# One gathered tile in twenty-four is built by ScalarE from columns of the node table, in both layers of a graph network

## The reference

```python
# layer 0, then x = layernorm(x + y)
m = relu(concat([x[dst], x[src], edge_attr, u[batch[dst]]]) @ W1.T + b1)
y = relu(concat([x, segment_sum(m, dst), u[batch]]) @ W2.T + b2)
# layer 1, then x = layernorm(x + y)
h = relu(concat([x[src], x[dst], edge_attr]) @ msg_w1 + msg_b1)
a = segment_mean(h @ msg_w2 + msg_b2, dst)
y = relu(concat([x, a]) @ upd_w1 + upd_b1) @ upd_w2 + upd_b2
```

## Time and profile before

| | us |
|---|---|
| median of 3 runs (lowest, highest) | 3929.26 (3928.97, 3930.61) |
| span of the profiled execution | 3929.8 |

### The profile page before, as it was taken

How to read it: one execution, slowest core, us unless ns; L and a number is a source line. 1 busy time by engine, 2 the same in 40 slices (tenths; PEclk the granted TensorE clock), 3 DMA queues, 4 the chain that set the end, 5 groups by cost and what they waited for, 6 DMA issues and landing times.

```text
span 3929.8 us, 45222 instructions
## 1 busy us (share of the span) xinstructions
PE 3229.0 (82%) x16881; PEld 2975.7 (76%) x16881; DVE 1583.8 (40%) x3640; ACT 590.4 (15%) x1017; POOL 2960.2 (75%) x3156
## 2 busy tenths in 40 slices
PE   6988888888788888888878888878888888888887
PEld 6877777777777777777778777777777777777776
DVE  6533334343444444444543333333433333333333
ACT  1211111111111111111111111111111111111111
POOL 7777777777777777777777777777777777777776
PEclk7755555565655556665665555555555555555556
DMA  7644444444444444445454444444444444444443
GB/s 261 200 138 134 135 136 143 132 133 139 148 139 149 149 149 147 147 147 154 131 158 135 133 131 124 135 139 136 139 136 141 139 142 137 140 135 141 142 142 100
DMA packets 257760, 563.18 MB, mean 143 GB/s; under 512 B 131254, under 2 KB 151713, under 8 KB 232572
## 3 DMA queue, kind: packets, MB, share of 16 engines
q1 hardware_dynamic: 132824, 332.20, 25.4%
q0 software_dynamic: 100032, 205.00, 19.8%
q10 hardware_dynamic: 24676, 23.01, 1.7%
HBM read 537.29 MB, written 22.66 MB: 142 GB/s over the span
## 4 chain that ended last, share of the span: by engine, by line
POOL 70%; issue 23%; DMA 4%; DVE 2%; PE 2%; ACT 0%; SPq 0%; POOLq 0%; DVEq 0%
POOL Qr L319 70%; DMA Qr<-tabQ,srcE 3%; DVE BIG L1405 1%; PE bank L1137 0%; DMA srcE<-in_srcL 0%; DVE BIG L1302 0%; PE bank L1119 0%; PE bank L1092 0%; DVE BIG L1392 0%; DMA tabQ<-BIG 0%; DVE BIG L1400 0%; PE bank L1051 0%; PE bank L1045 0%; DVE AC L609 0%; POOL Qr L325 0%
## 5 line engine op out<-in xcount | busy, mean ns | idle before, releaser
L319 POOL DMA_INDIRECT Qr<-tabQ,srcE x3094 | 2925.3, 945 | 942.9 <-issue 933.2
L1137 PE MATMUL bank<-BIG 128*128 128x42 f32 x6252 | 1379.0, 396 | 143.6 <-ACT BIG L1287 141.1
L1119 PE MATMUL bank<-wall,BIG 128*128 128x128 f32 x6252 | 1473.0, 410 | 19.1 <-DMA BIG<-tabP 19.1
L1137 PEld LDWEIGHTS bank<-BIG 128*128 128x128 f32 x6252 | 1307.5, 308 | 207.6 <-ACT BIG L1287 201.5
L1302 DVE TENSOR_TENSOR BIG<-bank,BIG 126x512 bf16<-126x512 f32 x782 | 539.3, 690 | 2264.7 <-DMA Qr<-tabQ,srcE 2254.8
L1119 PEld LDWEIGHTS bank<-wall,BIG 128*128 128x128 f32 x6252 | 1311.5, 309 | 23.8 <-issue 23.8
L1287 ACT ACTIVATE BIG<-BIG 128x512 f32<-128x512 f32 (+1 forms) x782 | 492.1, 629 | 3229.1 <-DVE BIG L1405 3220.4
L1124 PE MATMUL bank<-BIG 126*128 126x128 bf16 x3126 | 490.2, 295 | 506.5 <-DVE BIG L1302 396.7
L1124 PEld LDWEIGHTS bank<-BIG 126*128 126x128 bf16 x3126 | 342.0, 135 | 639.0 <-DVE BIG L1302 455.9
L1405 DVE TENSOR_TENSOR BIG<-bank,Qr 128x512 f32<-128x512 f32 (+1 forms) x782 | 532.7, 681 | 41.2 <-PE bank L1124 25.3
L1392 DVE TENSOR_TENSOR BIG<-bank,relE 128x168 f32<-128x168 f32 x782 | 252.6, 323 | 3.5 <-DMA Qr<-tabQ,srcE 3.5
(11 more groups left out here) (137 smaller groups left out, 609.9 us busy)
## 6 DMA issues: line engine op xcount, KB each, us to landing
BIG<-in_eaT SPq DMA_DIRECT2D x194, 1024.0 KB, 5.4
BIG<-in_dstR SPq DMA_DIRECT2D x194, 504.0 KB
Qr<-tabQ,srcE POOLq DMA_INDIRECT x3094
BIG<-tabP SPq DMA_DIRECT2D x526, 31.5 KB
tabP<-BIG ACTq DMA_DIRECT2D x22, 384.0 KB, 3.1
tabQ<-BIG ACTq DMA_DIRECT2D x17, 256.0 KB, 5.2
X<-in_xN SPq DMA_DIRECT2D x1, 3136.0 KB, 16.8
tabE<-BIG ACTq DMA_DIRECT2D x11, 256.0 KB, 2.3
```

The lines of the kernel that those rows point to most:

```text
L319: e.indirect_dma_start(Q[0:p, i % R_Q, j, :], None, table[:, :], bass.IndirectOffsetOnAxis(ap=srcE[0:p, g, j:j + 1], axis=0)).then_inc(f_q ...
L1119: e.matmul(bank[i % R_C][:, j * D:(j + 1) * D], f_eaT[:, k % R_EA, (g % LQ * J + j) * P:(g % LQ * J + j + 1) * P], wc[l], start=(j == 0), ...
L1137: last = e.matmul(sums[:, 0:W], M[:, i % R_M, j, :], S[:, hot(i), j, :], start=(j == 0 and first_of(i)), stop=(j == n - 1 and last_of(i)))
```

## The change

In every sixth group, the one at 6n + 10, POOL gathers only three of the four tiles (64 groups in layer 0, n = 0 to 63, and 63 in layer 1, n = 1 to 63: 127 gathers). For the fourth, ACT copies 128 single columns of `XT` (one for each edge's source) into a tile `XC` of 128 x 128, a sixth of them (21 or 22) behind the relu of each of the groups 6n to 6n + 5. The numbers of the columns lie in a new tile `colI`, are loaded into registers by groups, and each copy has its source offset in a register. `XC` is a ring of two. PE then multiplies `XC` by the weights `wq` into the fourth tile's part of its sum, DVE adds only three tiles of `Q`, and ACT applies relu to three tiles in `M` and separately from PE's bank to the fourth.

Since `XT` has to hold the old features until layer 0's last column is copied, `xt_copy` now writes the new ones into `AC[:, 0]`, where a finished unit's sums are no longer needed; PE's `q1` reads them there. `xt_move` copies them to `XT` on ACT, for units 0 to 10 two by two at groups 384 to 389 of layer 0 and for the last three ahead of group 0 of layer 1; the clearing of `AC[:, 0]` moves from `second` to `clear`, behind the moves. One small load (`colI`) is added at the start on ACT's queue, and `hidden` of layer 1 waits for the moves.

```diff
+MOVES = [(0, NG - 7 + u // 2) for u in range(NU - 3)] + [(1, 0)] * 3
+MOVED = 2
+COPIERS = ((6, 10),)
+TAKEN = [[[n * per + lead for n in range(NG) if n * per + lead < NG - 2 and n * per >= (0, MOVED)[l]] for l in range(2)]
+         for per, lead in COPIERS]
+R_X = 2
...
+        def gathered(i):
+            return tiles(i % NG) - (col_tile(i) is not None)
...
-                for j in range(tiles(g)):
+                for j in range(gathered(i)):
                     p = VP if g == NG - 1 and j == VJ else P
                     e.indirect_dma_start(Q[0:p, i % R_Q, j, :], None, table[:, :],
...
+            e.dma_start(colI[0:len(COL_ROWS), :], a["srcC"]).then_inc(s_bas, 16)
...
-                    last = e.matmul(bank[o][:, k * D:(k + 1) * D], XT[:, (b + k) * P:(b + k + 1) * P], wq[1], start=(k == 0), stop=(k == n - 1))
+                    last = e.matmul(bank[o][:, k * D:(k + 1) * D], AC[:, 0, (b + k) * P:(b + k + 1) * P], wq[1], start=(k == 0), stop=(k == n - 1))
...
                         e.wait_ge(u_qv, NU)
+                        e.wait_ge(s_mv, NU)
...
+                        if col_tile(i) is not None:
+                            h, c = col_tile(i)
+                            e.wait_ge(s_col[h], COPIERS[h][0] * (c + 1))
+                            e.matmul(bank[i % R_C][:, (J - 1) * D:J * D], XC[h][:, c % R_X, :], wq[l], start=False, stop=False)
                         e.wait_ge(v_st, i + 1)
...
-                e.copy(XT[:, b * P:(b + n) * P], bank[unit_bank(0, "x1t", u)][:, 0:n * P]).then_inc(u_tc, 1)
+                e.copy(AC[:, 0, b * P:(b + n) * P], bank[unit_bank(0, "x1t", u)][:, 0:n * P]).then_inc(u_tc, 1)
+
+            def xt_move(u):
+                b, n = UN[u]
+                e.wait_ge(u_tc, u + 1)
+                if u == 0:
+                    for k, (per, _) in enumerate(COPIERS):
+                        e.wait_ge(s_col[k], per * len(TAKEN[k][0]))
+                e.copy(XT[:, b * P:(b + n) * P], AC[:, 0, b * P:(b + n) * P]).then_inc(s_mv, 1)
...
+            def columns(l, g):
+                if col_piece(0, l, g) is None:
+                    return
+                c, row, lo, hi, new = col_piece(0, l, g)
+                if new and c >= R_X:
+                    e.wait_ge(v_C, col_group(0, c - R_X) + 1)
+                if new and c == len(TAKEN[0][0]):
+                    e.wait_ge(s_mv, NU)
+                _, at = nc.values_load_multi_w_load_instructions(
+                    colI[row:row + 1, lo:hi], engines=[mybir.EngineType.Activation], min_val=0, max_val=N - 1,
+                    skip_runtime_bounds_check_because="the source of an edge, which is a node")
+                for x in range(lo, hi):
+                    last = e.copy(XC[0][:, c % R_X, x:x + 1], XT[:, bass.ds(at[x - lo], 1)])
+                last.then_inc(s_col[0], 1)
...
                         e.wait_ge(v_tt, i + 1)
-                        m = M[:, i % R_M, 0:tiles(g), :].rearrange("p j d -> p (j d)")
-                        e.activation(m, m, ACT.Relu).then_inc(v_rl, 1)
+                        m = M[:, i % R_M, 0:gathered(i), :].rearrange("p j d -> p (j d)")
+                        last = e.activation(m, m, ACT.Relu)
+                        if col_tile(i) is not None:
+                            last = e.activation(M[:, i % R_M, J - 1, :], bank[i % R_C][:, (J - 1) * D:J * D], ACT.Relu)
+                        last.then_inc(v_rl, 1)
+                        columns(l, g)
...
-                if l == 0:
-                    e.memset(AC[:, 0, b * P:(b + n) * P], 0.0).then_inc(s_mz, 1)
+
+            def clear(u):
+                b, n = UN[u]
+                e.wait_ge(s_mv, u + 1)
+                e.memset(AC[:, 0, b * P:(b + n) * P], 0.0).then_inc(s_mz, 1)
...
-                        n = tiles(g - 1)
+                        n = gathered(i)
...
+                    for u in range(NU):
+                        if MOVES[u] == (l, g):
+                            clear(u)
```

More of the change, by code:

```diff
@@ L100, with col_tile, col_group, col_piece @@
 LAST = BASE[-1]
+MOVES = [(0, NG - 7 + u // 2) for u in range(NU - 3)] + [(1, 0)] * 3
[3 more added lines that the diff above has]
+         for per, lead in COPIERS]
+COL_ROW = [sum(len(TAKEN[x][0]) for x in range(k)) for k in range(len(COPIERS))]
+COL_ROWS = [i for t in TAKEN for i in t[0]]
+R_X = 2
+def col_tile(i):
+    l, g = divmod(i, NG)
+    for k in range(len(COPIERS)):
+        if l < 2 and g in TAKEN[k][l]:
+            return k, len(TAKEN[k][0]) * l + TAKEN[k][l].index(g)
+    return None
+def col_group(k, c):
+    return TAKEN[k][0][c] if c < len(TAKEN[k][0]) else NG + TAKEN[k][1][c - len(TAKEN[k][0])]
+def col_piece(k, l, g):
+    per, lead = COPIERS[k]
+    n, q = divmod(g, per)
+    if n * per + lead not in TAKEN[k][l]:
+        return None
+    return col_tile(l * NG + n * per + lead)[1], COL_ROW[k] + n, q * P // per, (q + 1) * P // per, q == 0
 ROWS = [2 + SPACED * (c - UPFRONT) for c in range(NC)]
@@ L169, in build @@
         srcR = sb("srcR", [P, RAW * J], I32)
+        colI = sb("colI", [P, P], I32)
+        XC = [sb(f"XC{k}", [P, R_X, P]) for k in range(len(COPIERS))]
         vsum = sb("vsum", [P, 1])
@@ L230, in build @@
         p1 = {n: sem(f"p1_{n}") for n in ("c", "hi", "r", "mid", "lo")}
+        s_col = [gs[1]["bt"], gs[1]["ct"]]
+        s_mv = gs[1]["bv"]
         s_mz, s_mean, s_ind, s_u, s_ru, s_meet = (sem(n) for n in ("s_mz", "s_mean", "s_ind", "s_u", "s_ru", "s_meet"))
@@ L307, in tiles @@
             return -(-VALID // P) if g == NG - 1 else J
+        def gathered(i):
+            return tiles(i % NG) - (col_tile(i) is not None)
         def q_count(i):
-            return 16 * sum(tiles(x % NG) for x in range(i % R_Q, i + 1, R_Q))
+            return 16 * sum(gathered(x) for x in range(i % R_Q, i + 1, R_Q))
         def gathers(e, l, g0, g1, table):
@@ L428, in start_scalar @@
                 raw_copy(e, r)
+            e.wait_ge(s_bas, 48)
             e.wait_ge(s_wl, 16)
@@ L467, in bases_to_rows @@
             def bases_to_rows():
-                e.wait_ge(s_bas, 32)
+                e.wait_ge(s_bas, 48)
                 link(e.tensor_reduce(wrow[:, :], third[:, :], AX, ALU.add))
@@ L625, in general_gpsimd @@
                 for r in range(PF):
-                    e.wait_ge(f_q[r], 16 * J)
+                    e.wait_ge(f_q[r], 16 * gathered(r))
             e.sem_inc(q["done"], 1)
@@ L1050, in q1 @@
                 for k in range(n):
-                    last = e.matmul(bank[3][:, k * D:(k + 1) * D], XT[:, (b + k) * P:(b + k + 1) * P], wp[1], start=False, stop=(k == n - 1))
+                    last = e.matmul(bank[3][:, k * D:(k + 1) * D], AC[:, 0, (b + k) * P:(b + k + 1) * P], wp[1], start=False, stop=(k == n - 1))
                 last.then_inc(p_c, 1)
@@ L1251, in rows_store @@
                 e.dma_start(node_rows(tabP[0], c), fP3[:, c % R_U, 0:CH[c][1], :]).then_inc(s_tabP[0][c % R_PT], 16)
+            def columns(l, g):
[12 more added lines that the diff above has]
+                last.then_inc(s_col[0], 1)
             for l in range(2):
                 for g in range(LAST + 11):
+                    for u in range(NU):
+                        if MOVES[u] == (l, g):
+                            xt_move(u)
                     if l == 0:
@@ L1585, in laid_out @@
         "srcL": srcp.astype(_np.int32).reshape(NGP, J, P).transpose(2, 0, 1).reshape(P, NGP * J),
+        "srcC": srcp.astype(_np.int32).reshape(NGP, J, P)[COL_ROWS, J - 1],
         "dstL": dstp.astype(_np.int32).reshape(NGP, J, P).transpose(2, 0, 1).reshape(P, NGP * J),
```

## The result

The changed kernel takes 4642.29 us (median of 4 runs, 4641.96 to 4647.36), the kernel before beside it 3929.47. The ratio is 1.182 (95% interval 1.180 to 1.183). I had forecast 3772 us and given the rival that ACT becomes the bound 7%. It did become the bound, through the register loads and not through the copies.

The account below looks back on a forecast made before the run. POOL's gathers, 1.250 us apart, were taken to bound the kernel: 3929.8 less 158.8 for 127 gathers plus 1.5 for the turn gives 3772.5, as median 3772 us. Forecast 3765 to 3779, range 3764 to 3805.

Parts of the forecast that it names:

- The load of 21 or 22 registers: In ACT's sum for a group: loading a piece's column numbers takes about 0.71 us, counted in full.
- that ACT stays below a group's 4.79 us: ACT's sum for a group: 4.22 us against 4.79, 88%, or 3.5 if the load runs under the relu.
- the slower case: Among the closing chances: the changed kernel is slower than the kernel before, 7%.
- The copies: In ACT's sum: one-column copies at 0.13 us each, 2.77 us a group, with 0.07 and 0.25 as ends.
- The gathers' saving: On POOL: 127 gathers fewer at 1.250 us each save 158.8 us, and nothing hides them.
- PE did not bind: On PE: 84% of a group's 4.79 us in layer 1, 88% busy in late layer 0; rival that it binds, 4%.
- ACT is the new bound: Rival on ACT: copies at their full 205 ns give 4060 to 4600 us; decided from 0.157 to 0.19 a copy; 7%.
- Delay against rate: Behind ACT's copies: the next relu starts up to 3.5 us late, a delay and no rate; POOL has 35 us.
- The turn: Between the layers: moves, clearings and PE's backlog delay the chain by -0.5 to +5 us, taken as 1.5.

Follow-up runs that it names:

- e5: The pieces of e1 with the column numbers stored one word later, so that no load starts at a multiple of 16 bytes: 5434.11 us.
- e1: The changed kernel with pieces cut at columns 0, 20, 40, 64, 84, 104, so each register load starts at a multiple of 16 bytes: 3778.24 us.
- e3: The changed kernel without register loads and with one copy of 21 or 22 fixed (wrong) columns for each piece: 3772.91 us.
- e2: The changed kernel with registers loaded once, at the first piece, and used by all copies (wrong columns): 3772.90 us.
- e4: The changed kernel with its loads kept but only two copies for each piece, all but the last column from fixed places: 3779.78 us.
- e7: Aligned pieces as in e1, but every fifth group short of a tile, 151 tiles in place of 127: 3744.54 us.
- e9: The changed kernel with every fourth group short of a tile (191 tiles), aligned pieces of 32 columns; three runs: 5537.19, 5417.29, third 4171.38 us.

## Why the prediction was wrong

**The step that failed** is "The load of 21 or 22 registers": "one register takes 306 ns, four 341, 12 ns for each more", so 0.71 us. Measured: 1.54 us for two loads in six and 4.66 to 4.90 for four, 3.70 on average. This is 3.0 us more in each of 762 groups, 2280 us of sequencer work. The step behind it failed with it: that ACT stays below a group's 4.79 us. With 0.71 us for the load the ledger's sum for a group is 3.0 us; with the measured load it is 6.0. The two lengths in the earlier trace rows were right; the slope was not one. Both loads of DVE start at a multiple of 16 bytes (`baseI` from a multiple of four on) and end within the same 16 bytes, so they could not show what the next four registers cost, nor what a start off the boundary costs. I carried a line through 1 and 4 on to 21, and gave this term no upper end, while I bounded the copies from both sides. With one, 0.306 x 21.3 = 6.5 us a group, the slower case would have had far more than its 7%.

On the same point, the Trainium skill's page Runtime: NRT & Kernel Launch, section "Instruction fetch mechanics", puts a register load at about 200 ns for each register. The page speaks of loads from device memory. Here, from the scratchpad, e5 shows 0.22 us for each unaligned register, near that figure, and e1 0.24 for four aligned ones, far below it.

**The copies** were right in kind and better than taken: 0.092 us from start to start for my 0.13; each lasts 187 ns and overlaps the next by 95, as the earlier trace rows had it (94). The register operation, 37 ns each on the sequencer, doesn't show in this distance, since the overlap in the earlier trace rows is of instructions without one.

```profile
L1316 ACTq FUSED_REGOPS  x16256: 37/37/43, 57.8 to 4621.8; - x199
L1316 ACT COPY XC<-XT x16256: 174/187/193, 57.9 to 4621.9; 128x1 f32 x199
```

By the Trainium skill's page VectorE: DVE Perf Modes, section "The TRN2 errata — SBUF-src ops pay a fixed extra latency per instruction", one column is an estimated (224 + 1) / 1.2 = 187.5 ns, and the trace agrees with 187. By the Trainium skill's page ScalarE: Activation LUTs, section "What ACT_TABLE_LOAD costs", neighbours overlap by 93 ns, and the trace agrees with 95.

**The gathers' saving** was right where ACT keeps up: e3 and e2 land on 3773, forecast 3772. Nothing else came in their way; PE did not bind, with 82% busy in e1 as before.

**The rival "ACT is the new bound"** named the engine and the side, with the wrong cause: it asked for copies of 0.157 us or more, and they take 0.092. The number that decides is the load's. That 4642 lies near the rival's 4060 to 4600 is chance, since its copies were priced at twice their time and its load at a fifth.

**Delay against rate.** That a late relu is a delay and no rate held as long as the sum fits: in e4 loads of 4.7 us stand in its way, and the time is 3780.

**The turn** I took for 1.5 us. By POOL's waits above their ordinary 0.30 us it was 2 in e3, 3 in e2 and 8 in e1 and e4, the most of it ahead of the 12 gathers of the partial table. In e1:

```profile
1884.06 0.96 POOL L355 DMA_INDIRECT Qr<-tabE,srcE  x1 [6.17 <-DVE BIG L1481]
```

I had looked at the last q store only, and it costs e1 another 2.2 us. The larger wait is for unit 11's store to `tabE`, ACT's, issued at 1881.55. The view names DVE, but the gather starts 2.51 us behind that store's issue, and in e3, where the store is issued at 1877.26, 2.52 us behind it. In e7 the wait is 1.8 us, with more work on ACT, so its size isn't ruled by ACT's load alone; what rules it stays open.

## What to carry to other kernels

Work on a sequencer (register loads, register operations) is in no busy share: ACT was 46% busy here and set the time. Count the sequencer as an engine of its own, and where a busy share is low while the chain lies on the engine and says "issue", look there first. Two lengths close together, 1 and 4 registers here, need not give the slope to 21. Bound each new term from both sides, the one that looks small too. And an engine that takes over work from the bound has to fit with the sum of all it does: here the loads and the copies were each free alone.

## What the runs showed of the hardware

- A register load from the scratchpad costs ACT's sequencer 0.09 us and 0.24 for each started four registers if it starts at a multiple of 16 bytes, else 0.04 and 0.22 for each register. Medians, unaligned: 4.44, 4.66, 4.88 and 5.32 us for 20, 21, 22 and 24 registers (changed kernel, e5); aligned: 1.29, 1.53, 1.75 and 2.01 for 20, 24, 28 and 32 (e1, e7, e9). A start at a multiple of 8 bytes alone doesn't help: columns 42 and 106 have it, and their loads take 4.88.
- Copies of one column with a register in the source's address start 0.092 us apart on ACT. No run has one-column copies without the register.
- Long straight code shows at the sequencer: the instruction queue moved 353 packets in place of 93, 8 KB each, and inside the pieces the sequencer stood still 244 times for 0.28 us, 68 us in all. From one of these standstills to the next there are 127 to 129 of ACT's instructions in 217 of 243 cases, and twice as many in the other 26. In e9's third run it is so in 338 and 30 of 368. So regular a distance fits a fetch of instructions in blocks; no run tests that cause by itself. The queue before and in the changed kernel (packets, MB, share of 16 engines):

```profile
q14 instruction: 93, 0.76, 0.1%
...
q14 instruction: 353, 2.89, 0.2%
```
